# Fewer columns per tap of the second set, and its row sums in four quarters

## What is computed

```
x = x + L0(gn(x)); x = x + L1(gn(x)); x = x + L2(gn(x)); x = x + L3(gn(x))

def L3(inputs, W1, b1, gamma, beta):          # K = 3
    centers = inputs[:, 1:-1, 1:-1]            # every inner pixel
    kernel  = (centers @ W1 + b1)              # 9 taps for each of them: K x K
    weighted = patches(inputs) * kernel        # its 3x3 neighbours, all channels, by its taps
    yout = scatter_add(weighted)               # each back to the neighbour's own place
    yn = (yout - mean) * rsqrt(var + 1e-3) * gamma + beta   # moments over all images and pixels
    return where(yn >= 0, yn, 0.3 * yn)
```

## Time and profile before

| | us |
|---|---|
| median of 3 runs | 881.46 |
| the three runs | 881.46, 883.37, 876.04 |
| the profiled execution's own time | 881.37 |
| its span, from the first to the last instruction | 879.3 |
| TensorE busy | 672.5 (76%) |
| VectorE busy | 559.7 (64%) |
| ScalarE busy | 544.7 (62%) |
| GpSimd busy | 244.7 (28%) |

### The profile page before, as it was taken

One profiled execution on the slowest core, in us unless ns is written; L12 is line 12 of the kernel. 1 busy time (PEld: TensorE's weight loads), 2 busy tenths in 40 slices (PEclk: granted clock), 3 DMA queues, 4 the chain that ended last, 5 costly groups with the idle time before them and its releaser, 6 DMA issues. The chain is left out here.

```text
span 879.3 us, 22794 instructions
## 1 busy us (share of the span) xinstructions
PE 672.5 (76%) x9584; PEld 433.4 (49%) x9584; DVE 559.7 (64%) x1149; ACT 544.7 (62%) x564; POOL 244.7 (28%) x285
## 2 busy tenths in 40 slices
PE   5477776489878889789887749968879979736673
PEld 4322222189766656555411129966656668213453
DVE  4557677599944334355589979974434446768871
ACT  4799999434355548698799824426545810646874
POOL 4511111276045500000000046305540000017881
PEclk9889999889989979799999969989998989658987
DMA  9532221000000000000000000000000000002777
GB/s 301 156 86 85 85 73 38 1 1 2 1 3 4 3 3 2 1 1 3 25 2 1 1 1 1 1 1 3 4 3 3 2 25 1 0 1 87 226 218 234
DMA packets 59908, 37.15 MB, mean 42 GB/s; under 512 B 1952, under 2 KB 59424, under 8 KB 59808
## 3 DMA queue, kind: packets, MB, share of 16 engines
q1 hardware_dynamic: 59808, 35.71, 13.5%
HBM read 18.93 MB, written 16.78 MB: 41 GB/s over the span
## 5 line engine op out<-in xcount | busy, mean ns | idle before, releaser
L733 ACT ACTIVATE work<-X,l0s 128x2048 f32<-128x2048 f32 (+2 forms) x80 | 138.5, 1763 | 4.9 <-POOLq L309 4.9
L748 ACT ACTIVATE work<-ps 128x2048 f32<-128x2048 f32 x64 | 121.1, 1892 | 23.0 <-PE ps L441 23.0
L441 PE MATMUL ps<-work,cst 32*32 32x512 f32 x2048 | 76.1, 620 | 38.4 <-ACT work L748 26.8
L767 ACT ACTIVATE work<-ps 128x512 f32<-128x512 f32 x80 | 47.8, 597 | 92.8 <-PE ps L518 92.8
L529 PE MATMUL ps<-cst,work 128*128 128x143 f32 x640 | 93.9, 291 | 1.2 <-ACT work L767 0.6
L529 PEld LDWEIGHTS ps<-cst,work 128*128 128x128 f32 x640 | 85.3, 195 | 1.6 <-issue 1.6
L1226 POOL TENSOR_TENSOR co<-mv,cst 128x1 f32<-128x1 f32 x7 | 1.3, 190 | 302.8 <-DVEq L309 250.5
L966 DVE TENSOR_TENSOR X<-X,ps 128x512 f32<-128x512 f32 x64 | 43.6, 682 | 59.7 <-PE ps L454 59.6
L454 PE MATMUL ps<-work,w2d 128*32 128x512 f32 x512 | 69.6, 612 | 2.2 <-ACT work L748 2.2
L785 ACT ACTIVATE work<-ps 128x520 f32<-128x520 f32 x64 | 38.7, 604 | 50.3 <-PE ps L578 50.1
L327 POOL TENSOR_SCALAR work<-X,co 128x2048 f32<-128x2048 f32 (+1 forms) x16 | 62.9, 3941 | 20.2 <-PE ps L518 19.8
(11 more groups left out here) (139 smaller groups left out, 1236.4 us busy)
## 6 DMA issues: line engine op xcount, KB each, us to landing
out<-work SPq DMA_DIRECT2D x64, 256.0 KB, 3.2
work<-x SPq DMA_DIRECT2D x16, 512.0 KB, 5.8
work<-x SPq DMA_DIRECT2D x32, 256.0 KB, 2.8
work<-choose SPq DMA_DIRECT2D x8, 128.0 KB, 2.7
cst<-consts SPq DMA_DIRECT2D x1, 1009.5 KB, 9.7
cst<-consts SPq DMA_DIRECT2D x1, 64.0 KB, 2.0
```

The costliest lines, as they stand in the source:

```text
L441: last = pe.matmul(ps[C * m:C * m + C, g, :], wg[rows, m, C * g:C * g + C], y_piece(i, j, m)[rows, :], start=True, stop=True)
L733: act.activation(o, x_in.rearrange("p (j n) -> p j n", n=BANK), ACT.Gelu, scale=l0s[:, at:at + 1], bias=l0s[:, at + MULTI:at + MULTI + 1]) ...
L748: act.activation(zb[:, k % ZDEEP, :, :], ps[:, 0:4, :], ACT.Gelu).then_inc(s_zs, 1)
```

## The change

WIDE becomes a pair: set 0 keeps 3 copies of the 36 columns (108), set 1 gets 2 (72). For set 1 the sum over rows, its copy, the turning and the copy of the turned are done in four quarters of 32 image columns (128 columns of s each). QUARTER_AT is [2, 5, 8, 10]: after these blocks the columns of a quarter are complete, and s_ub counts them. TensorE does the sum of quarter b one block later (behind the taps of blocks 3, 6 and 9), and its turning two blocks later (behind blocks 4, 7 and 10), for the first three quarters; the fourth follows at the end. VectorE does the copies in the same order. The sums go to bank 4 and the turned to bank 5, which the taps do not use. Each quarter's rearranged copy is one instruction. Spreading waits for all ten steps of s_ssb. Set 0's steps stay as they are, apart from losing their argument.

```diff
-WIDE = 3
+WIDE = (3, 2)
+QUARTER_AT = [-(-(32 * b + 32 - TB + 1) // TB) for b in range(3)] + [BLOCKS - 1]
...
-                o = pe.matmul(ps[:, 6 + t % 2, j * G * K9:(j + WIDE) * G * K9], X[:, f * PIX + w * H:f * PIX + (w + 1) * H],
-                              w9s.rearrange("p (o k) -> p o k", o=1).broadcast_to([P, WIDE, G * K9]),
+                o = pe.matmul(ps[:, 6 + t % 2, j * G * K9:(j + WIDE[f]) * G * K9], X[:, f * PIX + w * H:f * PIX + (w + 1) * H],
+                              w9s.rearrange("p (o k) -> p o k", o=1).broadcast_to([P, WIDE[f], G * K9]),
                               start=True, stop=True)
...
+            def sum_quarter(b):
+                pe.wait_ge(s_ub, b + 2)
+                for ki in range(3):
+                    last = pe.matmul(ps[:, 4, b * P:b * P + P], shift[:, ki, :],
+                                     U[:, ki, 32 * b:32 * b + 32, :].rearrange("p w g -> p (w g)"),
+                                     start=(ki == 0), stop=(ki == 2))
+                last.then_inc(s_smb, 1)
+
+            def turn_quarter(b):
+                pe.wait_ge(s_ssb, 2 * b + 3)
+                pe.transpose(ps[:, 5, b * H:b * H + H], s_rows[:, b * P:b * P + P], ident).then_inc(s_smb, 1)
...
-                for w in range(W):
-                    taps(s, w)
-                sum_rows(s)
-                turn_rows(s)
-
-                pe.wait_ge(s_ssb, 2 * s + 2)
+                for t in range(BLOCKS):
+                    for w in range(TB * t, min(TB * t + TB, W)):
+                        taps(s, w)
+                    for b in range(3):
+                        if t == QUARTER_AT[b] + 1:
+                            sum_quarter(b)
+                        if t == QUARTER_AT[b] + 2:
+                            turn_quarter(b)
+                sum_quarter(3)
+                turn_quarter(3)
+
+                pe.wait_ge(s_ssb, 10)
                 pe.wait_ge(s_sel, (s + 1) * TILES * 16)
...
-                if last_block:
+                if (t in QUARTER_AT) if f else last_block:
                     last.then_inc(s_ub, 1)
...
+            def store_quarter(b):
+                dve.wait_ge(s_smb, 2 * b + 3)
+                dve.tensor_copy(s_rows[:, b * P:b * P + P].rearrange("p (r j g) -> p r j g", r=TILES, g=G),
+                                ps[:, 4, b * P:b * P + P].rearrange("p (j r g) -> p r j g", r=TILES, g=G)).then_inc(s_ssb, 1)
+
+            def store_turned(b):
+                dve.wait_ge(s_smb, 2 * b + 4)
+                dve.tensor_copy(ST[:, (4 + b) * H:(5 + b) * H], ps[:, 5, b * H:b * H + H]).then_inc(s_ssb, 1)
...
                 for t in range(BLOCKS):
                     store_taps(s, t)
-                store_s(s, 0)
-                store_s(s, 1)
+                    for b in range(3):
+                        if t == QUARTER_AT[b] + 1:
+                            store_quarter(b)
+                        if t == QUARTER_AT[b] + 2:
+                            store_turned(b)
+                store_quarter(3)
+                store_turned(3)
```

More of the change, by code:

```diff
@@ L415, in taps, with sum_rows, turn_rows @@
                     o.then_inc(s_tb, 1)
-            def sum_rows(f):
-                pe.wait_ge(s_ub, f + 1)
+            def sum_rows():
+                pe.wait_ge(s_ub, 1)
                 for ki in range(3):
-                    last = pe.matmul(ps[:, 7, :], shift[:, ki, :], (U if f else U_b)[:, ki, :, :].rearrange("p w g -> p (w g)"),
+                    last = pe.matmul(ps[:, 7, :], shift[:, ki, :], U_b[:, ki, :, :].rearrange("p w g -> p (w g)"),
                                      start=(ki == 0), stop=(ki == 2))
                 last.then_inc(s_smb, 1)
-            def turn_rows(f):
-                pe.wait_ge(s_ssb, 2 * f + 1)
+            def turn_rows():
+                pe.wait_ge(s_ssb, 1)
                 for b in range(4):
-                    last = pe.transpose(ps[:, 6, b * H:b * H + H], (s_rows if f else s_rows_b)[:, b * P:b * P + P], ident)
+                    last = pe.transpose(ps[:, 6, b * H:b * H + H], s_rows_b[:, b * P:b * P + P], ident)
                 last.then_inc(s_smb, 1)
+            def sum_quarter(b):
[8 more added lines that the diff above has]
+                pe.transpose(ps[:, 5, b * H:b * H + H], s_rows[:, b * P:b * P + P], ident).then_inc(s_smb, 1)
             for s in range(NS):
@@ L487, in background @@
                         if u == SUM_AT:
-                            sum_rows(0)
+                            sum_rows()
                         if u == TURN_AT:
-                            turn_rows(0)
+                            turn_rows()
                         if u in PAIR_AT:
@@ L946, in store_taps, with store_s @@
                 last = dve.tensor_tensor(o, o, tap_of(2), ALU.add)
-                if last_block:
+                if (t in QUARTER_AT) if f else last_block:
                     last.then_inc(s_ub, 1)
-            def store_s(f, r):
-                dve.wait_ge(s_smb, 2 * f + r + 1)
+            def store_s(r):
+                dve.wait_ge(s_smb, r + 1)
                 if r == 0:
                     for k in range(TILES):
-                        by_tile = (s_rows if f else s_rows_b)[:, :].rearrange("p (b r j g) -> p b r j g", b=4, r=TILES, g=G)[:, :, k, :, :]
+                        by_tile = s_rows_b[:, :].rearrange("p (b r j g) -> p b r j g", b=4, r=TILES, g=G)[:, :, k, :, :]
                         src = ps[:, 7, :].rearrange("p (b j r g) -> p b r j g", b=4, r=TILES, g=G)[:, :, k, :, :]
@@ L957, in store_s @@
                 else:
-                    last = dve.tensor_copy(ST[:, f * 4 * H:(f + 1) * 4 * H], ps[:, 6, :])
+                    last = dve.tensor_copy(ST[:, 0:4 * H], ps[:, 6, :])
                 last.then_inc(s_ssb, 1)
+            def store_quarter(b):
[5 more added lines that the diff above has]
+                dve.tensor_copy(ST[:, (4 + b) * H:(5 + b) * H], ps[:, 5, b * H:b * H + H]).then_inc(s_ssb, 1)
             for s in range(NS):
@@ L999, in background @@
                         if u in (SUM_AT, TURN_AT):
-                            store_s(0, u - SUM_AT)
+                            store_s(u - SUM_AT)
                         if u in PAIR_AT:
```

## The result

| | before | after |
|---|---|---|
| median, range, runs | 882.29 us, 876.04 to 883.37, 4 runs | 901.72 us, 900.99 to 904.05, 4 runs |
| span of the profiled execution | 879.3 us | 898.7 us |
| stages 0 to 4 | 713.5 us | 710.4 us |
| stage 5 | 64.9 us | 90.8 us |
| output stage | 100.9 us | 97.5 us |

The ratio is 1.0242, with a 95% interval of 1.0192 to 1.0293: slower by 2.4%. The stages' times are worked out from the traces, as the distances between the points at which all engines have reached a stage's end; here the output stage includes the few steps for the moments. The interval lies wholly above 1, so the change is slower clear of the noise; whether by more than 2% stays open. Stage 5 alone is 26.0 us longer (25.97 before rounding).

What follows compares the result with a forecast made beforehand. It took 128x128 weight loads to bound the second set's taps. With the clock held at half, +25.55 us to the first spreading and +0.3 for that spreading gave +25.9, so 907.3 us; range 888 to 911.

Steps and rivals of the forecast that it cites:

- The load sets the pitch: Second set's taps: loading 128x128 weights, not columns, bounds each record, 0.112 us under the full clock, 0.213 under the half.
- The clock stays at the lower level with 72 columns: Second set's taps: the clock stays at 0.50 to their end, making 237 records longer, +24.1 us; 70%.
- Rival B: Second set's taps: back-to-back work raises the clock as before, only the quarters remain, 880.1 us; 17%.
- Rival C: Second set's taps: a quarter's sum over rows lifts the clock midway, 888.8 us, or 893 and 898 if later; 10%.
- Rival D: Second set's taps: the pitch goes by columns, VectorE becomes the bound, and the clock must rise too, 871 us; 3%.
- The sum for stage 5: From the second set's taps to the first spreading: starts at 777.5 instead of 751.95, +25.55 us.
- the tail: Last block's end to first spreading: last quarter's sum, turning and copies, 2.65 us under the half clock, 1.9 under the full.
- The quarters: Three quarters of sum and turning run beside the taps; under the full clock spreading starts at 750.6 instead of 751.95.
- The total: Whole kernel: +25.9 us in all, giving 907.3 us, a ratio of 1.029.
- the likeliest case: Second set: the clock is held at the lower level to the taps' end, 907.3 us with a spread of +-3; 70%.

Runs made afterwards that it cites:

- lift_then_72: The changed kernel, but the second set's first two blocks of taps stream 108 columns and the other nine 72; 880.97 us, ratio 1.0017 to before.
- cols_72_only: The kernel before with 72 columns a tap in the second set, sum over rows and turning left whole at the end; 905.66 us, ratio 1.0270 to before.
- quarters_36: The changed kernel with 36 columns a tap in the second set instead of 72; 903.09 us, ratio 1.0264 to before.
- quarters_108: The changed kernel with 108 columns a tap in both sets, so only the quarters remain; 872.47 us, ratio 0.9915 to before.

## Why the prediction was right, and what it mis-sized

*The load sets the pitch.* Right in its size: 0.213 us at 0.50 with 72 and with 36 columns, 0.112 at 1.00 with 108, 72 and 36. The rows of before gave 0.210 for the half clock and the prediction took 0.213 without saying why; the runs bear it out.

*The clock stays at the lower level with 72 columns.* Right, at 70% the least certain step. It rested on one comparison, with a stretch that TensorE streamed for 1.72 of each 2.67 us without a rise. It was a thin ground: in lift_then_72 the same 72 columns ran at 1.00, so how much is streamed doesn't settle the level by itself, and the level from which the taps start counts too. Here they start at 0.50, as in the earlier trace rows, so the forecast came out right without it. cols_72_only and quarters_36 show the lower level again, from the same start. Rival B, that back-to-back work is enough, fell with the 59.40 us of busy time at 0.50. The Trainium skill, "TensorE: Matmul & The Clock Gate", section "Why this matters for your kernels", advises to keep TensorE busy continuously. That doesn't hold here as far as busy means what the profile counts. The Trainium skill's same page, section LDWEIGHTS, gives a load the time of its columns over 1.2 GHz, 107 ns for 128. That agrees with the 0.112 us under the full clock and not with the 0.213 under the half. Rival C fell too: three sums of six dense records each, at 731.7, 748.4 and 765.2, raised nothing. Its later forms were priced wrongly: from one sum to the next there are three blocks of 12 taps, 72 records and not 36, so a rise at the second or third sum would have cost (72 + 7) x 0.102 = 8.1 us more each, about 897 and 905 us for 893 and 898. Both lie in the stated range. Rival D needed a pitch by columns and fell with the first step.

*The sum for stage 5.* Predicted +25.55 us to the first spreading, measured +25.64; the first spreading 2.13 us, predicted 2.09. Within it two small misses cancel: the last block ended 60.99 us behind the first matmul, 0.2 earlier than predicted, and the tail behind it took 774.43 - 771.49 = 2.94 us, predicted 2.65. In the tail the sum took 1.66 (1.5), the turning 0.49 (0.42) and the copies 0.30 (0.28).

*The quarters.* Right in size by quarters_108: 1.51 and 1.1 us in two pairs of profiles, where 1.35 was priced for the full clock.

*The total.* Predicted 907.3 us, a ratio of 1.029; measured 901.7 and 1.0242, which lies in the range. The mis-sized term is the one that was set to nothing: that all stages besides stage 5 take what they took. They took 6.5 us less in that profile: 3.1 in the stages before, whose code is untouched (they ended between 707.3 and 713.5 us over all fourteen profiles), and 3.4 in the output stage, which takes 97.5 to 105.0 us for the same code. The prediction allowed +-3 us for such shifts, and the miss is 5.6; the likeliest case's own spread, 904 to 910, doesn't hold the measured 901.7. It lies in the range only because the range takes in rival C, which didn't happen; that is luck. With the extra matmuls in both kernels the difference is 25.7 us, and the single later run of the changed kernel took 908.1.

*What stays open.* The gain of quarters_108 over before is 7.5 us, of which stage 5 explains 2.1 (1.8 by the second profiles). Its output stage was 97.6 us in both profiles and its eleven times lie between 869 and 875 us, so it seems to meet the short length regularly. The kernel before had 5 of 19 runs under 876 us beside it and 2 of the 32 later ones, and lift_then_72, with a short output stage in its profile (the shortest of its runs, 871.98 us), had most runs near 881. What decides whether a kernel meets it, by what comes ahead of the stage, was not found; keeping TensorE busy at its start did not shorten it. Nor was it found what moved the end of stage 4 between 707.3 and 713.5 us. And that 72 columns go on at the higher level but don't reach it is seen and not explained.

## What to carry to other kernels

Columns that look like waste can be what raises TensorE's clock: where a stream is bound by its weight loads, cutting the columns saves nothing and can leave the clock at half, so read the granted clock of the stretch before cutting, and price the cut at both levels. Here extra columns on the first 24 taps alone brought stage 5 from 90.8 to 64.8 us, for 62.8 with extra columns on all 128. And where a later stage has different lengths under the same code, compare stage by stage and over several profiles before a few microseconds are credited to an edit.

## What the runs showed of the hardware that was not expected

- The same taps can run at either level, by the level they start from: with 72 columns per load the clock stayed at 1.00 in lift_then_72 for some 25 us behind the last tap with 108 (the quarters' sums included), and at 0.50 for 59.4 us in the changed kernel, at the same place and with the same loads. With 36 columns behind the same start it fell to 0.50 after some 4 us.
- A load of 128x128 fp32 weights in a back-to-back stream takes 0.213 us under the half clock (72 and 36 columns streamed between) and 0.112 under the full one (108, 72 and 36).
- The rounds of the output stage have two forms: 9.02 us at 1.00, or 10.4 to 10.6 us with the clock falling once in each, and once a round had a fall, the following ones mostly had it too. By how many rounds have it, the stage is 97.5 to 105.0 us long over the fourteen profiles, a spread of nearly 1% of the kernel.
